# q and k of a decoder layer projected once to 128 rows, their 96-row stacks made on TensorE by selection matrices

## The chip, the cores and the metric

The kernel runs on one core of a Trainium2 chip. Five engines share the work, each with an instruction queue of its own that runs in program order: PE (TensorE, matmuls into PSUM), DVE (VectorE), ACT (ScalarE), POOL (GpSimd) and SP (SyncE, which here only issues DMAs). They wait for one another by semaphores. The metric is the device time of one execution in microseconds (us); lower is better.

## What is computed

One pre-norm decoder layer on x and ctx of shape (32, 128, 128): 32 batches of 128 tokens with 128 channels. All weights and tensors are fp32.

```
x = x + proj(causal_attention(layernorm(x)))       # 16 heads of 8 channels
x = x + Wo(cross_attention(layernorm(x), ctx))     # one head of 128
x = x + moe(layernorm(x))                          # 8 experts, top 2, one shared expert

# in the first line, with f a factor by position and channel (rotary):
q, k, v = split(x @ W_attn.T + b_attn)
q, k = q * f, k * f
att = softmax(mask(q @ k.T / sqrt(8)))
```

## The kernel before

**Stages and slots.** The 32 batches go through a software pipeline. A table, ORDER, lists the stages; each row has a name, how many batches it runs ahead of (or behind) the current slot, a part, and for some the remainder of the batch by four for which alone it runs. In slot s every engine goes through the table once and issues what it has to do for each stage. The table thus sets the order on all engines. Layernorm, the transposes of x, the projections of q and k and the routing are done for a group of four batches (512 tokens) at a time: group g's projections in slot 4g-2, its routing 11 slots behind. So the slots come in four kinds. In this text slot A is the one with the projections (s mod 4 = 2), B the next (which ends with the routing's `ranks`), then C and D (which has the layernorm of the next group on POOL). Behind the pipeline come the expert layers, from about 385 us on; the change does not touch them.

**q and k before.** A score needs products of fp32 precision from a faster format of 4 bytes with fewer bits (fp32r). Each value is therefore split into a rounded half (hi) and the rest (lo), and a head's 8 channels become 24 rows: hi, hi, lo for q against hi, lo, hi for k. Four heads make a stack of 96 rows (KR), and there are four stacks (NJ) for q and four for k. Before the change the three copies come from the weights: `wqk_hi` and `wqk_lo` hold every weight column three times.

- `project` (PE L636): eight per group, n = 0 to 7, each three matmuls (hi x hi, hi x lo, lo x hi) of 96 rows by 512 tokens into one of the four shared PSUM banks. DVE (L1090) adds the bias and multiplies by the factor into `t_qk`.
- `stacks` (ACT L884): one copy per batch, `t_qk` to `qk_stack`, which rounds.
- `stack_lo` (DVE L1101): two instructions per batch that turn the lo rows into t - hi. Then SP issues eight DMAs that spread the stacks of k and q into `k_slots` and `q_slots` (L415, L421), for which the score matmuls wait.

**Around it, per batch.** `scores` (PE L654, L655; DVE L1113 takes the row maximum), `turn_max`, `scores_t` (PE L670; ACT L896 takes the exponential; POOL L566 masks the result), `values` (PE L680, 32 small matmuls), `tall_sums` (PE L688 transposes, after ACT L902), `turn_y` (PE L694), `attn_out`, then the cross-attention (`turn_x2`, `xproject`, `xscores`, `turn_xprobs`, `xout`) and the norm for the experts (POOL L552, L554; PE L736).

**Banks.** The four shared PSUM banks are used in turn by all these stages. A stage names its bank in the table BANK; PE waits with `bank_free` until the last use of that bank has been read, and the reading engine counts it in `bank_drained`. Two stages with one bank that follow each other therefore wait for a copy.

## Time and profile before

| | |
|---|---|
| time, median of 3 runs | 591.26 us (588.47 to 596.85) |
| profiled execution, as a whole | 590.25 us |
| its span, first to last instruction | 588.3 us |
| mean granted clock of PE | 0.916 of full speed |
| start up to slot 2 | 0 to about 50 us |
| pipeline, with a period of 44.4 us per group from 123 us on | 50 to about 385 us |
| expert layers | 385 to 588 us |

The profile lists per engine the busy time, groups of instructions with their mean duration, the waits with the engine that ended them, and the chain of work that ended last. A matmul's duration has its latency in it; what one costs in a row of many is the distance from one start to the next, here called its pitch.

### The profile page before, as it was taken

What the parts mean: (1) busy time and instruction counts of PE and PEld (TensorE: products, weight loads), DVE (VectorE), ACT (ScalarE), POOL (GpSimd) and SP (SyncE); (2) the same over time, 40 slices, a digit from 0 to 9 for tenths busy, and PEclk for the clock granted to TensorE, in tenths of its full rate; (3) what the DMA queues carried; (4) which work ended last, traced back from release to release, by engine and by line L of the source; (5) the groups of instructions that cost most, each with busy time, mean ns of one, the idle gap of its engine ahead of it and who ended that gap; (6) DMA issues with size and microseconds to landing.
All of it is one profiled execution on the core that took longest, in us unless ns stands there. A gap on an engine that the chain in (4) does not pass through costs nothing.

```text
span 588.3 us, 12877 instructions
## 1 busy us (share of the span) xinstructions
PE 478.2 (81%) x3398; PEld 358.6 (61%) x3398; DVE 440.6 (75%) x1291; ACT 304.3 (52%) x927; POOL 352.0 (60%) x465
## 2 busy tenths in 40 slices
PE   4638899997887987987977987655699999999994
PEld 4415666665665655655755765434577777777783
DVE  4698989999889889889879875577446666556575
ACT  1213776856746746746746766534134444444440
POOL 7313575745767767767767786865135555555552
PEclk9959999998998998998998997956989999999997
DMA  7312121221221221221221220511112222222185
GB/s 207 96 46 54 45 60 47 59 58 33 62 60 46 60 61 48 59 62 48 57 66 46 62 75 10 172 55 58 55 47 79 79 74 74 79 70 78 55 261 174
DMA packets 66780, 43.15 MB, mean 73 GB/s; under 512 B 9020, under 2 KB 63656, under 8 KB 66712
## 3 DMA queue, kind: packets, MB, share of 16 engines
q1 hardware_dynamic: 61654, 33.01, 22.1%
q0 software_dynamic: 4320, 8.99, 4.6%
q8 instruction: 32, 0.52, 0.4%
q10 hardware_dynamic: 738, 0.33, 0.2%
q14 instruction: 36, 0.29, 0.2%
HBM read 17.36 MB, written 12.09 MB: 50 GB/s over the span
## 4 chain that ended last, share of the span: by engine, by line
PE 55%; DVE 16%; issue 12%; POOL 7%; SPq 4%; ACT 4%; DMA 2%; DVEq 0%; POOLq 0%; ACTq 0%
PE ps_scores L811 9%; PE ps_shared L636 8%; PE ps_shared L680 5%; PE ps_shared L828 4%; PE ps_scores L654 3%; PE ps_scores L655 3%; PE ps_scores_t L670 2%; PE ps_shared L819 2%; PE ps_scores_t L765 2%; POOL probs L566 2%; PE ps_scores L765 2%; PE ps_shared L779 2%; POOL xs L559 2%; SPq L415 2%; PE ps_shared L699 1%
## 5 line engine op out<-in xcount | busy, mean ns | idle before, releaser
L566 POOL TENSOR_SCALAR_AFFINE_SELECT probs<-probs 128x512 f32<-128x512 f32 x128 | 91.8, 736 | 62.1 <-ACT probs L896 60.9
L586 POOL DMA_INDIRECT ys<-ctx_t,t_qk x71 | 68.5, 965 | 75.6 <-ACT ctx_t L994 71.5
L1113 DVE TENSOR_REDUCE negmax<-ps_scores 128x4 f32<-128x512 f32 x128 | 82.6, 679 | 8.8 <-PE ps_scores L655 8.7
L559 POOL DMA_INDIRECT xs<-xrow,posu x64 | 70.6, 1104 | 19.6 <-issue 11.9
L896 ACT ACTIVATE probs<-ps_scores_t 128x512 f32<-128x512 f32 x128 | 72.8, 593 | 18.3 <-PE ps_scores_t L670 18.0
L655 PE MATMUL ps_scores<-k_slots,qk_stack 96*128 96x512 f32 x128 | 77.4, 634 | 0.0
L811 PE MATMUL ps_scores<-wide,qk_stack 128*128 x213 | 69.9, 438 | 7.0 <-DVE vst L1300 2.9
L654 PE MATMUL ps_scores<-causal,ident 128*128 128x512 bf16 x128 | 53.1, 415 | 14.0 <-DMA k_slots<-qk_stack 11.8
L1306 DVE COPY probs<-ps_shared 128x256 f32<-128x256 f32 x71 | 30.1, 424 | 45.6 <-issue 22.9
L670 PE MATMUL ps_scores_t<-wide,qk_stack 97*128 97x512 f32 x128 | 61.7, 508 | 0.3 <-ACT probs L896 0.2
L1101 DVE SCALAR_TENSOR_TENSOR qk_stack<-qk_stack,lo_rows,t_qk 96x512 fp32r<-96x512 f32 x64 | 58.6, 953 | 1.7 <-ACT qk_stack L884 1.7
L1090 DVE SCALAR_TENSOR_TENSOR t_qk<-ps_shared,bqk,ropes 96x512 f32<-96x512 f32 x64 | 45.5, 743 | 8.4 <-PE ps_shared L636 8.3
L811 PEld LDWEIGHTS ps_scores<-wide,qk_stack 128*128 128x128 f32 x213 | 36.4, 193 | 23.0 <-issue 19.0
L989 ACT ACTIVATE vst<-ps_scores 128x256 f32<-128x256 f32 x71 | 27.3, 384 | 42.5 <-PE ps_scores L811 40.1
L680 PE MATMUL ps_shared<-probs,vst 128*32 128x128 f32 x1024 | 35.8, 281 | 14.9 <-issue 13.9
L828 PE MATMUL ps_shared<-wd,probs 128*128 x284 | 43.8, 277 | 0.1
L680 PEld LDWEIGHTS ps_shared<-probs,vst 128*32 128x32 f32 x1024 | 27.5, 113 | 22.2 <-issue 22.1
L902 ACT ACTIVATE yu<-ps_shared 128x512 f32<-128x512 f32 x32 | 19.1, 598 | 37.7 <-PE ps_shared L680 37.7
L984 ACT ACTIVATE qk_stack<-ps_scores_t 128x128 fp32r<-128x128 f32 x71 | 19.7, 278 | 35.9 <-PE ps_scores_t L803 24.3
L884 ACT ACTIVATE qk_stack<-t_qk 96x1024 fp32r<-96x1024 f32 x32 | 33.3, 1044 | 9.1 <-DVE t_qk L1090 9.1
L828 PEld LDWEIGHTS ps_shared<-wd,probs 128*128 128x128 f32 x284 | 37.7, 193 | 0.3 <-issue 0.3
L1300 DVE SCALAR_TENSOR_TENSOR vst<-vst,t_qk,ps_scores 128x256 f32<-128x256 f32 x71 | 33.5, 471 | 2.2 <-ACT vst L989 2.2
(227 smaller groups left out, 1222.0 us busy)
## 6 DMA issues: line engine op xcount, KB each, us to landing
k_slots<-qk_stack SPq DMA_DIRECT2D x128, 48.0 KB
wide<-qk_stack SPq DMA_DIRECT2D x128, 48.0 KB
t_qk<-xs SPq DMA_DIRECT2D x71, 66.0 KB
wide<-ys SPq DMA_DIRECT2D x8, 512.0 KB, 7.9
ctx_t<-in_ctx SPq DMA_DIRECT2D x32, 64.0 KB, 2.1
out_x<-res SPq DMA_DIRECT2D x8, 256.0 KB, 3.1
ys<-ctx_t,t_qk POOLq DMA_INDIRECT x71
wd<-in_L_ffn_w_down SPq DMA_DIRECT2D x8, 128.0 KB, 3.3
```

What stands on the lines that cost most here:

```text
L559: pool.indirect_dma_start(out=xs, out_offset=bass.IndirectOffsetOnAxis(ap=posu[:, g % 2, k, u:u + 1], axis=0), in_=xrow[:, g % 2, k, u, :] ...
L566: pool.affine_select(out=part, in_=part, compare_op=ALU.is_ge, fill=0.0, base=0, pattern=[[0, HJ], [1, T]], channel_multiplier=-1).then_in ...
L586: pool.indirect_dma_start(out=ys, out_offset=bass.IndirectOffsetOnAxis(ap=xload_i[:, i % XL, C + 1:C + 2], axis=0), in_=ybuf[:, i % 4, :], ...
L654: pe.matmul(PS[j % 2][:], ident16[:], causal[:].rearrange("p a t -> p (a t)"), start=True, stop=False)
L655: pe.matmul(PS[j % 2][:], qk_stack[0:KR, b % 4, j, :], k_slots[:, b % 2, j].rearrange("p a t -> p (a t)"), start=False, stop=True)\
L670: pe.matmul(PT[j % 2][:], qk_stack[0:KR + 1, b % 4, NJ + j, :], q_slots[:, b % 4, j].rearrange("p a t -> p (a t)"), start=True, stop=True) ...
L680: mm = pe.matmul(bank[VW * i:VW * (i + 1), j * T:(j + 1) * T], vst[:, b % 4, h, :], probs[:, b % 2, h, :], start=True, stop=True, skip_gro ...
L811: mm = pe.matmul(PS[i % 2][:], a[:, i % 4, :], m[:, bass.ds(e, 1), :].rearrange("p a f -> p (a f)"), start=(r == 0), stop=(r == 2))
L828: mm = pe.matmul(PM[i % 2][:, 0:C], xhT[:, i % 3, f * 128:(f + 1) * 128], wd[:, bass.ds(e, 1), f, :].rearrange("p a c -> p (a c)"), start= ...
L896: act.activation(probs[:, b % 2, j * HJ:(j + 1) * HJ, :].rearrange("p a t -> p (a t)"), PT[j % 2][:], ACT.Exp)\
L1101: ins = dve.scalar_tensor_tensor(out=part, in0=part.bitcast(fp32), scalar=lo_rows[:, k:k + 1], in1=t_qk[0:KR, cs, u * T:(u + 1) * T], op0= ...
L1113: dve.reduce_max(negmax[:, b % 2, j * HJ:(j + 1) * HJ], PS[j % 2][:].rearrange("p (i t) -> p i t", i=HJ), axis=AX.X, negate=True).then_inc ...
```

## The change

q and k are projected once, to 128 rows each (16 heads by 8 channels): two projections per group instead of eight. DVE adds the bias and multiplies by the factor as before, now 128 rows at a time. The new stage `halves` splits the result for the whole group: ACT copies it rounded to `qk_hi`, DVE subtracts to `qk_lo`. The new stage `select` makes the stacks on PE: for a pair of batches (256 tokens) and each quarter j of the rows, two matmuls for q and two for k multiply 32 rows of `qk_hi` and `qk_lo` by constant matrices of zeros and ones (`picks`), which place every channel in its three rows. ACT copies the bank to `qk_stack`, which has six places now instead of four. `stacks` and DVE's part of `stack_lo` are gone; SP's part waits for the copies of `select`. Pair 0 of a group is selected in slot A, pair 1 in slot B. The weights are no longer tripled at the start; DVE makes `picks` there instead, and one more DMA is issued.

```diff
 ORDER = [
     ("turn_x", 2, None, 0),
     ("turn_ffn", -7, None, None),
-    ("stacks", 1, None, 0),
     ("rstd_x", 3, None, 0),
     ("scores_t", -2, 2, None),
     ("turn_max", -1, None, None),
+    ("project", 2, 0, 0),
     ("scores_t", -2, 3, None),
+    ("project", 2, 1, 0),
     ("xscores", -5, None, None),
     ("router", -7, None, None),
...
     ("project_v", 1, None, 2),
+    ("halves", 2, 0, 0),
     ("turn_y", -3, None, None),
-    ("project", 2, 5, 0),
+    ("halves", 2, 1, 0),
...
     ("values", -2, None, None),
-    ("project", 2, 1, 0),
-    ("project", 2, 3, 0),
     ("project_v", 2, None, 3),
-    ("project", 2, 6, 0),
+    ("select", 2, 0, 0),
+    ("select", 3, 0, 2),
+    ("select", 2, 1, 0),
+    ("select", 3, 1, 2),
...
-        "router": 1, "turn_x2": 0, "ranks": 0, "project": (0, 1, 1, 3, 3, 3, 2, 2)}
+        "router": 1, "turn_x2": 0, "ranks": 0, "project": (1, 3), "select": (1, 3, 2, 0)}
...
             def stack_lo(b):
 
-                w.ge(stacked, b + 1)
+                for j in range(NJ):
+                    w.bank_read(("select", b // 2 * 2, j))
...
             def project(g, n):
 
-                col = (n + NJ) % (2 * NJ)
+                col = 1 - n
...
-                    mm = pe.matmul(bank[0:KR, :], a[:, col, :], m[:, 0, :], start=(k == 0), stop=(k == 2))
+                    mm = pe.matmul(bank[:], a[:, col, :], m[:, 0, :], start=(k == 0), stop=(k == 2))
                 mm.then_inc(put_bank(("project", g, n)), 1)
+
+            def select(b, j):
+                bank = w.bank_free(("select", b, j))
+                w.ge(qk_split, 2 * (b // GB + 1))
...
+                r, cs = slice(32 * j, 32 * (j + 1)), slice(b % GB * T, (b % GB + 2) * T)
+                for k in range(2):
+                    part = bank[0:KR, k * 2 * T:(k + 1) * 2 * T]
+                    for n, m in enumerate((qk_hi, qk_lo)):
+                        mm = pe.matmul(part, picks[r, k, n].rearrange("p i a d -> p (i a d)"), m[r, k, cs], start=(n == 0), stop=(n == 1))
+                mm.then_inc(put_bank(("select", b, j)), 1)
...
-            def stacks(b):
-
-                u = b % GB
-                w.bank_read(("project", b // GB, 7))
-                w.ge(scored_t, NJ * (b - 3))
-                act.activation(qk_stack[0:KR, b % 4], t_qk[0:KR, :, u * T:(u + 1) * T], ACT.Copy).then_inc(rounded, 1)
+            def halves(g, n):
+                w.bank_read(("project", g, n))
+                for j in range(NJ):
+                    w.bank_read(("select", GB * g - 2, j))
+                act.activation(qk_hi[:, 1 - n, :], qk[:, 1 - n, :], ACT.Copy).then_inc(rounded[n], 1)
+
+            def select(b, j):
+
+                bank, drain = w.bank_filled(("select", b, j))
+                w.ge(scored_t, NJ * (b - RING + 2))
+                s = b % RING
+                act.activation(qk_stack[0:KR, s:s + 2, j::NJ, :].rearrange("p u k t -> p k u t"),
+                               bank[0:KR, :].rearrange("p (k u t) -> p k u t", k=2, u=2), ACT.Copy).then_inc(drain, 1)
...
+            def halves(g, n):
+                w.bank_read(("project", g, n))
+                w.ge(rounded[n], g + 1)
+                for j in range(NJ):
+                    w.bank_read(("select", GB * g - 2, j))
+                dve.tensor_tensor(qk_lo[:, 1 - n, :], qk[:, 1 - n, :], qk_hi[:, 1 - n, :].bitcast(fp32), ALU.subtract).then_inc(qk_split, 1)
+
             def stack_lo(b):
-
-                u = b % GB
-                w.ge(rounded, b + 1)
-                for k, cs in enumerate((slice(0, NJ), slice(NJ, 2 * NJ))):
-                    part = qk_stack[0:KR, b % 4, cs, :]
-                    ins = dve.scalar_tensor_tensor(out=part, in0=part.bitcast(fp32), scalar=lo_rows[:, k:k + 1],
-                                                   in1=t_qk[0:KR, cs, u * T:(u + 1) * T], op0=ALU.mult, op1=ALU.add)
-                ins.then_inc(stacked, 1)
```

Quarters 2 and 3 of `select` stand in ORDER where `project` 0 and 4 stood, around `xproject` and `scores_t`. Some tensors share memory now (`early`, `late`); no stage moves by that.

**PE, start of a slot A.** In these rows `xn1` and `early` are the normalized x, `ps_shared0` to `ps_shared3` the four banks, and the brackets name the semaphores waited for. Before:

```order
L624 MATMUL ps_shared2<-ident,xn1 128x128 x3
L736 MATMUL ps_shared1<-ident,xrow 128x128 [waits xn3_ready,bank_drained1]
L670 MATMUL ps_scores_t0<-wide,qk_stack 128x512 [waits exped]
L662 MATMUL ps_shared3<-ident,negmax 16x128 [waits maxed,bank_drained3]
L670 MATMUL ps_scores_t1<-wide,qk_stack 128x512 [waits exped]
L719 MATMUL ps_shared2<-xcT,qa 128x128 [waits bank_drained2]
L741 MATMUL ps_shared1<-wrT,x3T 128x9 [waits bank_drained1]
L654 MATMUL ps_scores0<-causal,ident16 128x512 [waits k_slotted2,maxed]
L655 MATMUL ps_scores0<-k_slots,qk_stack 128x512
L694 MATMUL ps_shared1<-ident,yn 128x128 [waits bank_drained0,bank_drained1]
L636 MATMUL ps_shared3<-xT_hi,wqk_hi 96x512 [waits xT_split,bank_drained3]
```

The same place of the change:

```order
L626 MATMUL ps_shared2<-ident,early 128x128 x3
L750 MATMUL ps_shared1<-ident,xrow 128x128 [waits xn3_ready,bank_drained1]
L684 MATMUL ps_scores_t0<-wide,qk_stack 128x512 [waits exped]
L676 MATMUL ps_shared3<-ident,negmax 16x128 [waits maxed,bank_drained3]
L638 MATMUL ps_shared1<-xT_hi,wqk_hi 128x512 [waits xT_split,bank_drained1]
L638 MATMUL ps_shared1<-xT_lo,wqk_hi 128x512
L638 MATMUL ps_shared1<-xT_hi,wqk_lo 128x512
L684 MATMUL ps_scores_t1<-wide,qk_stack 128x512 [waits exped]
L638 MATMUL ps_shared3<-xT_hi,wqk_hi 128x512 [waits xT_split,bank_drained3]
L638 MATMUL ps_shared3<-xT_lo,wqk_hi 128x512
L638 MATMUL ps_shared3<-xT_hi,wqk_lo 128x512
L733 MATMUL ps_shared2<-xcT,qa 128x128 [waits bank_drained2]
```

The first matmul that waits for the split x (`xT_split`) stood behind `turn_y` (L694) and stands now two stages behind the transposes of x, ahead of the cross-attention scores (L719, now L733).

**PE, end of a slot A.** From the score matmuls to the transposes of the sums (L688, now L702). Before, where a projection is one row of its three:

```order
L655 MATMUL ps_scores1<-k_slots,qk_stack 128x512
L636 MATMUL ps_shared0<-xT_hi,wqk_hi 96x512 [waits xT_split,bank_drained0]
...
L712 MATMUL ps_shared2<-xcT,wA 128x128 [waits bank_drained0,bank_drained2]
L713 MATMUL ps_shared2<-wM,xcT 128x128
L670 MATMUL ps_scores_t0<-wide,qk_stack 128x512 [waits q_slotted1,max_placed,exped]
L636 MATMUL ps_shared3<-xT_hi,wqk_hi 96x512 [waits xT_split,bank_drained3]
...
L730 MATMUL ps_shared3<-cm,xprobsT 128x128 [waits bank_drained1,bank_drained3]
L670 MATMUL ps_scores_t1<-wide,qk_stack 128x512 [waits exped]
L688 MATMUL ps_shared0<-ident,yu 128x128 [waits bank_drained0]
```

The same place of the change, of each quarter's four matmuls the first two:

```order
L669 MATMUL ps_scores1<-k_slots,qk_stack 128x512
L650 MATMUL ps_shared2<-qk_hi,picks 96x256 [waits qk_split,bank_drained2]
L650 MATMUL ps_shared2<-qk_lo,picks 96x256
...
L726 MATMUL ps_shared2<-xcT,wA 128x128 [waits bank_drained0,bank_drained2]
L727 MATMUL ps_shared2<-wM,xcT 128x128
L684 MATMUL ps_scores_t0<-wide,qk_stack 128x512 [waits q_slotted1,max_placed,exped]
L650 MATMUL ps_shared0<-qk_hi,picks 96x256 [waits qk_split,bank_drained0]
L650 MATMUL ps_shared0<-qk_lo,picks 96x256
...
L744 MATMUL ps_shared3<-cm,xprobsT 128x128 [waits bank_drained1,bank_drained3]
L684 MATMUL ps_scores_t1<-wide,qk_stack 128x512 [waits exped]
L702 MATMUL ps_shared0<-ident,late 128x128 [waits bank_drained0]
```

The third quarter fills bank 2, and the next stage, `xproject` (L726), waits for bank 2; the fourth fills bank 0, for which the transposes (L702) wait two stages later. A slot B has the same rows now.

**DVE, start of a slot A.** Before:

```order
L1083 TENSOR_TENSOR xT_lo<-xT,xT_hi 128x512 [waits xhi_done,bank_drained2]
L1144 TENSOR_REDUCE xneg<-ps_shared2 128x1 [waits bank_drained2,bank_filled2]
L1165 MAX mx8<-ps_shared1 128x8 [waits bank_filled1]
L1168 MAX_INDEX ix8<-mx8,ps_shared1 128x8 [waits topped]
L1101 SCALAR_TENSOR_TENSOR qk_stack<-qk_stack,lo_rows,t_qk 96x512 [waits rounded]
L1113 TENSOR_REDUCE negmax<-ps_scores0 128x4 [waits bank_drained3,scored]
L1090 SCALAR_TENSOR_TENSOR t_qk<-ps_shared3,bqk,ropes 96x512 [waits stacked,bank_filled3]
```

The same place of the change:

```order
L1106 TENSOR_TENSOR xT_lo<-early,xT_hi 128x512 [waits xhi_done,bank_drained2]
L1112 SCALAR_TENSOR_TENSOR early<-ps_shared1,bqk,ropes 128x512 [waits bank_filled1]
L1112 SCALAR_TENSOR_TENSOR early<-ps_shared3,bqk,ropes 128x512 [waits bank_filled3]
L1165 TENSOR_REDUCE xneg<-ps_shared2 128x1 [waits bank_drained2,bank_filled2]
L1186 MAX mx8<-ps_shared1 128x8 [waits bank_filled1]
L1189 MAX_INDEX ix8<-mx8,ps_shared1 128x8 [waits topped]
L1134 TENSOR_REDUCE negmax<-ps_scores0 128x4 [waits bank_drained3,scored]
L1122 TENSOR_TENSOR qk_lo<-early,qk_hi 128x512 [waits bank_drained3,bank_drained2,bank_drained1,bank_drained0,rounded0]
```

Both bias adds of the group (L1112) stand now between the split of x and the row maximum of the cross-attention (L1144, now L1165) and the router's index (L1168, now L1189), which PE's `turn_y` waits for through its bank; the stack adds (L1101) are gone.

## Rows read from the trace of the kernel before

**Rows 1.** The page, busy us, share of the span and instructions by engine

```profile
PE 478.2 (81%) x3398; PEld 358.6 (61%) x3398; DVE 440.6 (75%) x1291; ACT 304.3 (52%) x927; POOL 352.0 (60%) x465
```

**Rows 2.** Slots A to D of one group, all engines; columns below

```profile
204.80:220.70 15.90, 12.87 (x97) 9.29 (x96) 12.44 (x29) 7.11 (x22) 10.71 (x16) 1.00 0.24 60
220.70:231.20 10.50, 7.22 (x70) 5.10 (x68) 9.67 (x36) 7.75 (x23) 8.78 (x12) 0.97 0.19 48
231.20:240.70 9.50, 9.40 (x71) 7.13 (x72) 8.86 (x39) 6.27 (x19) 4.78 (x7) 0.68 0.21 53
240.70:249.20 8.50, 7.45 (x72) 5.46 (x71) 7.16 (x20) 6.71 (x24) 7.78 (x9) 1.00 0.24 60
```

The columns are from:to, length, busy us (instructions) of PE, PEld, DVE, ACT and POOL, PE's granted clock, the DMA share and GB/s.

**Rows 3.** The chain that ended last: start, us, engine, output, line, count

```profile
217.89 2.11 PE ps_shared L636 x9
```

**Rows 4.** PE in order of time: start, us, operation, [idle before, its end]

```profile
222.65 0.33 PE L694 MATMUL ps_shared<-ident,yn 128*128 128x128 f32 x1 [0.21 <-DVE ix L1168]
...
224.88 1.08 PE L680 MATMUL ps_shared<-probs,vst 128*32 128x128 f32 x32 [0.31 <-issue]
...
231.26 0.18 PE L747 MATMUL ps_shared<-selb,tri 128*128 128x32 bf16 x1 [2.70 <-DVE cum L1191]
...
251.48 0.30 PE L736 MATMUL ps_shared<-ident,xrow 128*128 128x128 f32 x1 [1.58 <-POOL xrow L554]
251.88 0.48 PE L670 MATMUL ps_scores_t<-wide,qk_stack 97*128 97x512 f32 x1
...
256.63 1.08 PE L680 MATMUL ps_shared<-probs,vst 128*32 128x128 f32 x32 [1.28 <-issue]
```

**Rows 5.** The same chain further on, in another group

```profile
329.19 0.44 PE ps_shared L688 x4
```

**Rows 6.** Groups by line and shape, whole span: busy us, mean ns, idle before

```profile
L614 PE MATMUL ps_shared<-woT,probs 128*128 128x128 f32 x2 | 0.8, 501 | 0.3 <-DVE wpT L1051 0.3
L616 PE MATMUL ps_shared<-rows,one_row 1*128 1x128 f32 x2 | 0.8, 497 | 0.0
L636 PEld LDWEIGHTS ps_shared<-xT_lo,wqk_hi 128*96 128x96 f32 x64 | 10.7, 168 | 3.5
L1101 DVE SCALAR_TENSOR_TENSOR qk_stack<-qk_stack,lo_rows,t_qk 96x512 fp32r<-96x512 f32 x64 | 58.6, 953 | 1.7 <-ACT qk_stack L884 1.7
L1090 DVE SCALAR_TENSOR_TENSOR t_qk<-ps_shared,bqk,ropes 96x512 f32<-96x512 f32 x64 | 45.5, 743 | 8.4 <-PE ps_shared L636 8.3
L884 ACT ACTIVATE qk_stack<-t_qk 96x1024 fp32r<-96x1024 f32 x32 | 33.3, 1044 | 9.1 <-DVE t_qk L1090 9.1
L902 ACT ACTIVATE yu<-ps_shared 128x512 f32<-128x512 f32 x32 | 19.1, 598 | 37.7 <-PE ps_shared L680 37.7
```

**Rows 7.** DVE in order of time, start of the next slot A

```profile
252.00 0.68 DVE L1083 TENSOR_TENSOR xT_lo<-xT,xT_hi 128x512 fp32r<-128x512 f32 x1
```

**Rows 8.** All engines in order of time, 339 to 351 us

```profile
339.95 2.15 DVE L1101 SCALAR_TENSOR_TENSOR qk_stack<-qk_stack,lo_rows,t_qk 96x512 fp32r<-96x512 f32 x2
...
340.66 1.94 POOL L566 TENSOR_SCALAR_AFFINE_SELECT probs<-probs 128x512 f32<-128x512 f32 x2
...
348.87 1.22 POOL L566 TENSOR_SCALAR_AFFINE_SELECT probs<-probs 128x512 f32<-128x512 f32 x2
```

**Rows 9.** SP's DMA issues in order of time, 28 to 70 us

```profile
29.53 3.47 SPq L415 DMA_DIRECT2D k_slots<-qk_stack  x4
...
35.51 0.78 SPq L421 DMA_DIRECT2D wide<-qk_stack  x1
38.43 3.25 SPq L415 DMA_DIRECT2D k_slots<-qk_stack  x4
...
56.76 3.25 SPq L421 DMA_DIRECT2D wide<-qk_stack  x4
...
62.12 0.57 SPq L429 DMA_DIRECT2D wide<-max_rows  x1
63.30 3.71 SPq L415 DMA_DIRECT2D k_slots<-qk_stack  x4
```

More of the change, by code:

```diff
@@ L603, in _ @@
             pe.transpose(PM[1][:, 0:C], wsq[:, 4, :], ident[:])
-            pe.wait_ge(dve_step, 1)
-            for k in range(2 * NJ):
-                pe.matmul(PM[1][0:KR, 2 * C + k:2 * C + k + 1], brow[:, k, :], one_row[:, 0:1], start=True, stop=True)
             pe.transpose(PM[1][:, C:C + NE], wr[:], ident[0:NE, 0:NE]).then_inc(filled[1], 1)
@@ L901, in values @@
                 w.bank_read(("tall_sums", b - 1))
[L902 removed]
+                act.activation(yu, bank[:], ACT.Copy).then_inc(drain, 1)
             def turn_y(b):
```

132 lines of the change are left out of this document (68 added, 64 removed).

## The prediction, made before the change had run

> **What bounds it now.** I read the page's busy line first [rows 1]: PE is busy for 81% of the span and DVE for 75%, so neither is full, and the share alone tells nothing. Then the span by stretches. From 123 to 301 us the same pattern returns every 44.4 us, once per group of four batches, so I cut one group into its four slots [rows 2]: A (15.9 us, which holds all eight projections), B (10.5, which holds the routing), C (9.5) and D (8.5). DVE is the engine with the most work in the group (12.44 + 9.67 + 8.86 + 7.16 = 38.1 of 44.4 us). The change takes about 10 us of that away, and the question is what those 10 us now hold up.
>
> The chain that ended last and the waits of PE give the answer, slot by slot. In A, PE runs its projections back to back [rows 3], and its two long waits are 1.58 us at the start, for POOL's normalized rows, and 1.28 us before the values matmuls [rows 4]; there POOL's mask of the probabilities is the late one. In B it waits 0.21 us for DVE and 0.31 us before the values, and then 2.70 us for the running counts of the routing, a chain of small DVE instructions [rows 4]. C has no wait of note: PE is busy for 9.40 of 9.5 us, at a mean granted clock of 0.68, that is, partly at the lower level of 1.2 GHz after the 2.70 us of idleness [rows 2]. In D POOL is busy for 7.78 of 8.5 us [rows 2]. So DVE lies on the chain with short latencies and not with its total, and the two stages that the change takes from it, the add of the bias and the second half of the stacks, are hardly on it.
>
> **PE's work.** A projection costs 2.11 / 9 = 0.234 us per matmul of 512 columns [rows 3]. A group loses 18 of its 24, 4.2 us, all in slot A. It gains 32 matmuls of 256 columns (two pairs of batches, four quarters, four matmuls each), 16 in A and 16 in B. No row has 256 columns. From below: 128 columns take 0.44 / 4 = 0.11 us [rows 5]. From above: on the straight line between 0.11 and 0.234 they take 0.15. Half of the 512-column price is 0.117, so I take 0.13: 2.1 us in A, 2.1 us in B, 4.2 per group, between 3.5 and 4.8. That they multiply only 32 rows should make no difference: a matmul over one row (L616) took 497 ns where one over 128 rows (L614) took 501 [rows 6]. So PE's total stays as it is, but 2.1 us move from A to B.
>
> One price could be much worse, that of the weight loads, since each of the 32 matmuls has a matrix of its own. The projections show loads of 96 columns of 168 ns each [rows 6], and yet a pitch of 0.234, which leaves no room for them: they ran under the matmul ahead. The Trainium skill, "TensorE: Matmul & The Clock Gate", Part 3, The mechanism, says that a weight load overlaps a running matmul only where the two use different row groups. By that rule all four matmuls of a quarter, which share one row group, would pay their loads openly. The trace does not agree for the projections, which fill all rows and still hide theirs.
>
> **New waits in A and B.** (i) The projections now stand near the start of A. Their input, the low half of x, is ready at 252.00 + 0.68 = 252.68 [rows 7], while PE would reach the first at 251.88 [rows 4]: 0.8 us of wait, and queued behind it are score matmuls and the cross-attention scores. (ii) DVE's two bias adds (743 ns each [rows 6]) now stand ahead of the row maximum and the router's index, for which the next transpose on PE waits. I put this wait at 0.8 instead of 0.2, so +0.6; nothing if PE is late itself, 1.5 if both adds are waited for in full. (iii) The third quarter and the next stage, xproject, use the same PSUM bank, with nothing between them. PE must wait until the matmul has drained (about 0.25, since a matmul of 512 columns is 0.48 us long [rows 4] at a pitch of 0.234) and ACT has copied the bank, 598 ns for 128x512 [rows 6]: 0.85 us. (iv) The fourth quarter and the transposes of the sums share a bank too; between them PE has 0.45 us of work, but ACT has an exponential ahead of the copy, so 0.65 us. (v) The 1.28 us that A waits for POOL goes: PE now comes later than POOL.
>
> Slot A: -4.2 + 2.1 + 0.8 + 0.6 + 0.85 + 0.65 - 1.3 = -0.5 us. Slot B: + 2.1 + 0.85 + 0.65, less the 0.5 of its two short waits (0.21 and 0.31), which are gone when DVE and POOL have less to do there: +3.1 us. The 2.70 of the routing stay, since that chain begins behind the transposes and is not touched. C stays: nobody is waited for.
>
> **What DVE's relief gives.** It shows in one place. With the stack add beside it (339.95 to 342.10 us) a pair of POOL's masks takes 1.94 us; in the next slot, where there is none, 1.22 [rows 8]. In D POOL is the bound, and one such pair lies on the chain: -0.7 us. The remaining 8 adds of 953 ns and 6 of 743 per group were covered by PE. What replaces them on DVE (two adds, two subtractions of about 0.7) lies in A.
>
> ACT trades four copies of 1.04 us for two of 0.6 and eight of 0.6 [rows 6], +1.8 us per group. It is busy for 7.11 of 15.9 us in A and 7.75 of 10.5 in B [rows 2], so this is hidden but for (iii) and (iv); without the cover it would cost 11 us over six groups.
>
> **The first slots.** Up to 80 us the issues of SP bound the kernel, 8 copies per batch of 0.8 us each. SP lies idle from 36.29 (35.51 + 0.78) to 38.43, until DVE has added batch 1's stack, and from 60.01 to 62.12 and 62.69 to 63.30 [rows 9]. The stacks of two batches now come together and early, without DVE: 2.1 + 2.7 = about -5 us. The first issue at 29.53 moves little (a shorter weight split, but four drained banks to wait for). Behind the last group, slot 30 gains the 0.7 us of POOL.
>
> **Sum.** Seven groups have an A and a B with this work; the first lies in the stretch that SP bounds. Six groups from slot 6 on: 6 x (-0.5 + 3.1 - 0.7) = +11.4; start -5; end -0.7; together +5.7. The profiled execution took 590.25 us as a whole (span 588.3), 1.0 under the median of 591.26; 590.25 + 5.7 gives 596.
>
> **Rivals.**
> *Faster: DVE was the bound after all.* The relief would then show in every slot and not in D alone, and the waits (i) and (ii) would be absorbed. Price: 0.7 more in A, B and C each, and 0.8 + 0.6 in A; 3.5 per group, 21 in all less what B counts already (0.5 x 6): 18, so 578. For it: DVE has the most work of all in the group, and POOL's pair shows that it disturbs others. Against: only short DVE pieces lie on the chain. It decides from two further slots on that shorten by 0.7.
> *Slower: the drains are longer.* If ACT has one earlier copy in hand when the third or fourth quarter is full, each of the four waits per group grows by 0.6: 2.4 x 6 = 14 more, 610. For it: copies of two quarters and the values stand right ahead. Against: by my count ACT is free some 0.3 us before. It decides once these waits pass 1.2 us.
> *Slower: the loads are in the open.* 32 x 0.168 = 5.4 us per group, over all seven groups 38 more: 634. For it speaks that 256 columns (0.12 us) are shorter than a load of 168 ns; against it, that transposes of 128 columns, with loads of 128 columns, keep a pitch of 0.11 [rows 5]. The rule of the Trainium skill named above would lead here.
>
> **Chances.** The forecast has 0.56, with a range of its own from 588 to 604. The faster rival has 0.2, the longer drains 0.16, the open loads 0.08. Two per cent, which is about what a measurement of this kernel can tell from no change, is 579.4 to 603.1. Most of the faster rival lies under it (0.17); both slower ones lie above, with a little of the forecast's tail (0.25); 0.58 remains. The range from 579 to 613 takes in the bounds of the 256-column price (0.7 x 6 = 4 us either way) and of (ii), and leaves out the open loads and half of the faster rival.
>
> **What would show it.** In the profile after: slot B of a group grows from 10.5 to some 13.6 us, A and C keep their lengths, D loses 0.7. PE's idle time ahead of xproject and of the transposes of the sums ends with ACT's copies of the stacks, at about 0.85 and 0.65 us. The matmuls with the selection matrices start 0.13 us apart. SP has no gap of 2 us at 36. DVE's load per group falls to about 28 us. The prediction is wrong if B keeps its length (the drains are hidden), if C falls below 9 us, or if the granted clock drops in A or B ahead of the routing, for which no row here gives a price.

## The result, and the profile after

| | before | the change |
|---|---|---|
| median, side by side on one chip | 591.73 us (4 runs) | 606.69 us (603.88 to 610.03, 4 runs) |
| profiled execution, as a whole | 590.25 us | 603.88 us |
| its span | 588.3 us | 602.1 us |

The ratio is 1.025, with an interval from 1.015 to 1.034: slower, by 15 us, though the first comparison alone does not tell whether by more than 2 per cent. A second one, on another chip, gave 609.43 against 593.08, 1.033 (1.025 to 1.040). Medians are those of all executions, while ratios leave out the ones that lie in a slower state. The forecast was 596 with a range of its own from 588 to 604, and 579 to 613 over all cases. The time lies in the wide range and outside the narrow one.

The line of the profile that answers to [rows 1], busy us, share of the span and instructions by engine, of the change:

```profile
PE 492.3 (82%) x3494; PEld 365.1 (61%) x3494; DVE 368.7 (61%) x1198; ACT 321.4 (53%) x975; POOL 335.4 (56%) x465
```

DVE is busy for 72 us less and PE for 14 us more, although PE's work was to stay as it is (at the lower clock a matmul of 512 columns is 0.63 us long and not 0.40, and the change has more of that, see below).

For the comparison by slots I cut at the transposes of the expert norm (L736 before, L750 after), which are easy to find in both traces. First a group of before on this cut, slots A, B, C, D; the columns are those of [rows 2]; the clock is the third number from the end.

```profile
251.48:265.08 13.60, 12.17 (x90) 8.79 (x91) 12.12 (x28) 5.35 (x18) 8.51 (x12) 1.00 0.22 56
265.08:275.73 10.65, 7.31 (x73) 5.24 (x72) 9.83 (x36) 7.70 (x23) 8.78 (x12) 0.96 0.18 47
275.73:285.11 9.38, 9.35 (x71) 7.04 (x70) 8.74 (x39) 6.33 (x20) 4.77 (x7) 0.68 0.22 55
285.11:295.82 10.71, 8.09 (x76) 5.90 (x75) 7.43 (x22) 8.42 (x27) 9.94 (x13) 1.00 0.25 64
```

The same view of the change, two of its groups:

```profile
168.12:182.43 14.31, 12.82 (x89) 9.28 (x90) 8.62 (x24) 8.81 (x24) 8.21 (x12) 0.82 0.21 55
182.43:197.40 14.97, 11.97 (x89) 8.48 (x89) 7.48 (x32) 8.51 (x24) 8.29 (x12) 0.73 0.16 44
197.40:205.79 8.39, 8.36 (x69) 6.33 (x69) 7.22 (x35) 5.38 (x19) 4.24 (x7) 0.77 0.18 49
...
262.57:275.75 13.18, 10.96 (x88) 7.37 (x89) 8.52 (x24) 8.74 (x24) 8.25 (x12) 1.00 0.21 57
275.75:288.42 12.67, 9.61 (x90) 6.62 (x88) 7.54 (x31) 8.29 (x25) 8.29 (x12) 1.00 0.18 48
288.42:299.05 10.63, 9.00 (x71) 6.84 (x69) 7.93 (x37) 5.36 (x19) 4.24 (x7) 0.68 0.21 57
299.05:309.04 9.99, 8.10 (x77) 5.91 (x76) 5.50 (x20) 7.59 (x26) 9.21 (x13) 1.00 0.20 54
```

and slot A of its other groups from 120 us on:

```profile
120.01:135.61 15.60, 12.52 (x90) 8.61 (x89) 8.92 (x24) 9.75 (x27) 5.93 (x10) 0.89 0.18 48
215.77:229.83 14.06, 12.67 (x89) 8.91 (x90) 8.62 (x24) 8.81 (x24) 8.29 (x13) 0.83 0.19 51
309.04:323.62 14.58, 12.51 (x89) 8.64 (x89) 8.48 (x24) 8.73 (x24) 8.20 (x12) 0.88 0.18 49
```

Before, all groups are alike. After, they differ, and the granted clock tells which is which. In the second group A and B run at the full 2.4 GHz: A is 0.42 us shorter than before, B 2.02 longer. In the first one the clock is 0.82 in A and 0.73 in B, and they are 0.7 and 4.3 longer, but C is 1.0 shorter there and 1.2 longer in the second: B and C together are 23.36 and 23.30. D is 0.7 shorter.

The waits of PE over three groups of the change (168 to 307 us): us in total, times, longest.

```profile
PE ps_shared L761 <- DVE cum L1212: 6.5, 3, 2.2
PE ps_shared L750 <- POOL xrow L555: 4.7, 3, 1.6
PE ps_shared L726 <- ACT qk_stack L904: 4.1, 6, 0.7
PE ps_shared L708 <- DVE ix L1189: 2.5, 4, 1.6
PE ps_shared L638 <- DVE xT_lo L1106: 2.2, 3, 0.7
PE ps_shared L694 <- issue: 1.0, 3, 0.3
```

Lines three and five are new: `xproject` waits for the copy of the third quarter, 0.68 us in every slot A and B; the first projection for the split of x, 0.7 us once per group. `turn_y` waited for the router's index before, too, for 1.5 us over three groups, now for 2.5. The wait ahead of the values (L694, before L680), 7.5 us over three groups before, is 1.0.

Where the clock falls is seen in stretches of 1 us, at the start of the slot A from 215.77 us (first two) and at its end (last two):

```profile
217.77:218.77 1.00, 1.00 (x5) 0.82 (x4) 0.68 (x1) 0.45 (x1) 0.83 (x2) 0.74 0.04 8
218.77:219.77 1.00, 1.00 (x5) 0.81 (x5) 0.31 (x2) 0.15 (x1) 0.97 (x2) 0.50 0.19 49
...
227.77:228.77 1.00, 1.00 (x7) 0.60 (x5) 0.12 (x1) 1.00 (x3) 0.31 (x1) 0.86 0.00 0
228.77:229.77 1.00, 1.00 (x5) 0.85 (x5) 0.71 (x3) 0.69 (x2) 0.36 (x2) 0.50 0.00 0
```

Ahead of the first fall PE had waited 1.56 us for POOL and 0.71 for the split of x; ahead of the second, 0.68 for the third quarter's copy. Then it works at 1.2 GHz (0.50) though it has no idle time. Added up over 100 to 350 us, the granted clock was at the lower level for 34 us before (one stretch per group, behind the routing) and for 61 us after (up to three per group); in the profile of the second comparison it was 48. That the waits bring the fall about is a guess at this point.

### The profile page after: what moved, and what is told of

It is laid out like the page before. It is cut to its first block, busy times and chain, and to the rows that moved or that the text cites. A ratio compares the mean times of both kernels' runs of the same rounds, so it can differ in the third digit from the quotient of the medians.

```text
span 602.1 us, 13119 instructions
## 1 busy us (share of the span) xinstructions
PE 492.3 (82%) x3494; PEld 365.1 (61%) x3494; DVE 368.7 (61%) x1198; ACT 321.4 (53%) x975; POOL 335.4 (56%) x465
## 4 chain that ended last, share of the span: by engine, by line
PE 62%; DVE 12%; ACT 7%; issue 7%; POOL 5%; DMA 3%; SPq 3%; DVEq 0%; ACTq 0%; POOLq 0%
PE ps_scores L825 10%; PE ps_shared L694 5%; PE ps_scores_t L684 4%; PE ps_shared L842 4%; PE ps_scores L668 4%; PE ps_shared L650 4%; PE ps_scores L669 4%; PE ps_shared L638 3%; ACT qk_stack L904 3%; PE ps_shared L702 2%; PE ps_scores L779 2%; PE ps_shared L833 2%; PE ps_scores_t L779 2%; PE ps_shared L726 2%; PE ps_shared L793 1%
## 5 line engine op out<-in xcount | busy, mean ns | idle before, releaser
L567 POOL TENSOR_SCALAR_AFFINE_SELECT probs<-probs 128x512 f32<-128x512 f32 x128 | 81.8, 653 | 72.4 <-ACT probs L917 71.9
L1134 DVE TENSOR_REDUCE negmax<-ps_scores 128x4 f32<-128x512 f32 x128 | 85.2, 686 | 46.6 <-PE ps_scores L669 46.2
L590 POOL DMA_INDIRECT ys<-ctx_t,late x71 | 68.4, 964 | 72.5 <-ACT ctx_t L1015 69.8
L560 POOL DMA_INDIRECT xs<-xrow,posu x64 | 66.8, 1044 | 19.7 <-issue 11.8
L684 PE MATMUL ps_scores_t<-wide,qk_stack 97*128 97x512 f32 x128 | 64.8, 529 | 0.5 <-issue 0.3
L694 PE MATMUL ps_shared<-probs,vst 128*32 128x128 f32 x1024 | 37.2, 289 | 4.0 <-issue 3.3
L904 ACT ACTIVATE qk_stack<-ps_shared 96x512 fp32r<-96x512 f32 x64 | 35.8, 592 | 7.8 <-PE ps_shared L650 7.6
L1175 DVE SCALAR_TENSOR_TENSOR res<-ps_shared,xinv,late 128x128 f32<-128x128 f32 x32 | 11.2, 350 | 43.5 <-PE ps_shared L744 42.7
L545 POOL TENSOR_SCALAR xn<-late,mv,rs 128x128 f32<-128x128 f32 x32 | 25.4, 793 | 21.7 <-ACT rs L934 21.6
L923 ACT ACTIVATE late<-ps_shared 128x512 f32<-128x512 f32 x32 | 19.1, 597 | 30.3 <-PE ps_shared L694 30.3
L694 PEld LDWEIGHTS ps_shared<-probs,vst 128*32 128x32 f32 x1024 | 28.1, 115 | 11.3 <-issue 8.9
L573 POOL TENSOR_TENSOR late<-late,bias 128x128 f32<-128x128 f32 x32 | 14.6, 456 | 35.9 <-DVE late L1155 35.6
```

Of the source, the lines that this page charges most:

```text
L560: pool.indirect_dma_start(out=xs, out_offset=bass.IndirectOffsetOnAxis(ap=posu[:, g % 2, k, u:u + 1], axis=0), in_=xrow[:, g % 2, k, u, :] ...
L567: pool.affine_select(out=part, in_=part, compare_op=ALU.is_ge, fill=0.0, base=0, pattern=[[0, HJ], [1, T]], channel_multiplier=-1).then_in ...
L590: pool.indirect_dma_start(out=ys, out_offset=bass.IndirectOffsetOnAxis(ap=xload_i[:, i % XL, C + 1:C + 2], axis=0), in_=ybuf[:, i % 4, :], ...
L684: pe.matmul(PT[j % 2][:], qk_stack[0:KR + 1, b % RING, NJ + j, :], q_slots[:, b % 4, j].rearrange("p a t -> p (a t)"), start=True, stop=Tr ...
L694: mm = pe.matmul(bank[VW * i:VW * (i + 1), j * T:(j + 1) * T], vst[:, b % 4, h, :], probs[:, b % 2, h, :], start=True, stop=True, skip_gro ...
L904: act.activation(qk_stack[0:KR, s:s + 2, j::NJ, :].rearrange("p u k t -> p k u t"), bank[0:KR, :].rearrange("p (k u t) -> p k u t", k=2, u ...
```

## The experiments

All comparisons are with the kernel before on the same chip; "the change" stands at 606.7 in the expectations.

**Banks of the third and fourth quarter.** Nothing then fills these banks before ACT has copied them.

```diff
-        "router": 1, "turn_x2": 0, "ranks": 0, "project": (1, 3), "select": (1, 3, 2, 0)}
+        "router": 1, "turn_x2": 0, "ranks": 0, "project": (1, 3), "select": (1, 3, 1, 1)}
```

> The third and fourth quarter of select fill bank 1 (free since the first quarter was copied) in place of banks 2 and 0, so that neither xproject nor the transposes of the sums wait for a copy of a quarter; all else as in the change. Theory A, the drains: of the 606.7 us, each pair of quarters costs 0.68 us ahead of xproject and 0.31 ahead of the transposes of the sums, 2.0 us per group, and these go: 7 x 2.0 = 14 less, 593. Theory B, the clock: the short waits also bring TensorE's granted clock down in slots A and B; then the low stretches that begin behind xproject's wait (about 180 and 228 us in the profile of the change) go as well and the time falls below 590. Theory C, ACT is the limit of this section (its copies, the exponential and the two copies of xproject follow each other without a gap from 273.7 to 275.2 us): the wait only moves, to the exponential or to the next use of bank 1, and less than 5 us are gained, 602 or more.

Measured: 594.67 us, ratio 0.998 (0.993 to 1.002). So two numbers brought back 12 us by the medians and some 16 by the ratios; single executions run from 586.3 to 599.9, and the profiled one is the slowest. Slots A, B, C of one group:

```profile
258.65:271.46 12.81, 11.94 (x87) 8.44 (x89) 8.27 (x23) 8.46 (x24) 8.25 (x12) 0.87 0.21 59
271.46:283.59 12.13, 9.39 (x88) 6.64 (x88) 7.64 (x32) 8.52 (x25) 8.32 (x12) 1.00 0.18 50
283.59:294.14 10.55, 9.13 (x71) 6.80 (x70) 7.95 (x37) 5.39 (x19) 4.24 (x7) 0.68 0.22 59
```

Slot B is 11.8 to 12.1 us in the five groups from 120 us on, at a clock of 0.98 or more. Against the 12.67 of the change at full clock that is 0.5 less: the 0.68 ahead of `xproject` are gone, and the wait for the routing is 0.2 longer (2.4 us against 2.2). Against the change's other groups (13.5 to 15.0) it is 1.3 to 2.8 less, and these falls of the clock in B are gone, as theory B has it. But they had cost little: B and C together are 22.5 to 23.4 us in all five groups of the change, whether the clock fell in B or not, since C is the shorter behind a fall. Here they are 20.4 to 22.7. In the mean over these groups B and C give 1.4 us and A 1.3 (14.3 to 13.1), 2.7 per group, against the 2.0 of theory A. The time does not decide between theory A (593) and theory B (below 590): 12 us back make 594.7 and 16 make 590.7. The slots show the direct waits as the larger part. Theory C, ACT as the limit, falls. The low stretch in slot A stays (0.87 here, in three of five groups), so the drains are not its cause.

**The projections behind the router.**

```diff
-    ("project", 2, 0, 0),
     ("scores_t", -2, 3, None),
-    ("project", 2, 1, 0),
     ("xscores", -5, None, None),
     ("router", -7, None, None),
+    ("project", 2, 0, 0),
+    ("project", 2, 1, 0),
...
-        "router": 1, "turn_x2": 0, "ranks": 0, "project": (1, 3), "select": (1, 3, 2, 0)}
+        "router": 1, "turn_x2": 0, "ranks": 0, "project": (0, 3), "select": (1, 3, 2, 0)}
```

> The two projections stand behind the router and use banks 0 and 3 in place of 1 and 3, so that PE reaches them after the cross-attention scores, when the split of x is done; all else as in the change. Theory A, direct waits alone: the 0.74 us for the split of x go, and of the 0.60 for the router's index 0.4: 1.1 per group, 7 groups: 8 less, 599. Theory B, the clock: in the change the first low stretch of slot A begins right behind these waits (218 us); without them the granted clock of slot A is 1.00 in all groups, which gives up to 1 us more per group: 592. Against both: the halves come later, and the first quarter waits for DVE's qk_lo by up to 1 us; then nothing is gained, 605 to 608.

Measured: 597.07 us, ratio 1.008 (1.004 to 1.011), 9.6 us less than the change. Slots A and B of two groups:

```profile
261.16:273.21 12.05, 10.76 (x88) 7.58 (x90) 8.67 (x24) 8.62 (x24) 8.49 (x12) 1.00 0.22 61
273.21:285.87 12.66, 9.61 (x88) 6.62 (x88) 7.52 (x31) 8.26 (x25) 8.28 (x12) 0.97 0.18 50
305.29:318.00 12.71, 11.51 (x88) 8.41 (x89) 8.80 (x24) 8.76 (x24) 8.45 (x12) 0.91 0.21 56
318.00:332.88 14.88, 11.88 (x87) 8.46 (x88) 7.37 (x30) 8.45 (x24) 8.29 (x12) 0.73 0.16 42
```

At full clock A is 12.05 us, against 13.18: the 1.1 of theory A, to the tenth. Theory B was too bold: A has 1.00 in two of five groups, 0.91 in the other shown and 0.83 in another, and where the clock holds out in A it can still fall in B, where the drains are untouched (14.88 at 0.73).

**Both edits.** No new lines.

> The edits of the banks (bank 1 for the third and fourth quarter) and of the projections (behind the router, banks 0 and 3) together. Apart they gave 12.0 and 9.6 us of 606.7. If each takes away a wait of its own and the low stretch of the clock behind it, they add up: 585, and slots A and B show a granted clock of 0.95 or more. If the low stretch is brought about by what is left (the wait for POOL's row at the start of a slot A, that of the routing), it stays, and the two together give 590 to 593.

Measured: 588.32 us, ratio 0.997 (0.993 to 1.001): 18 of the 22 us that they gave apart. B is 11.8 to 12.1 at 1.00 throughout, but A still has a low stretch in three of five groups, here in that from 209.66 us:

```profile
209.66:221.74 12.08, 11.82 (x88) 8.47 (x90) 8.20 (x23) 8.43 (x24) 8.21 (x12) 0.86 0.22 59
```

The only wait that the trace shows in that slot is the 1.56 us for POOL's row. Before the change the same wait stood at the same place [rows 4], and the clock of A stayed at 1.00. Why it falls now is not settled: in these rows the slot differs in more than one thing. What the two edits gained lies nearly all in A (11.8 us in the mean over five groups, 14.3 in the change); B and C together are 22.2 to 22.9.

**All quarters on the same rows.** Quarters two to four repeat the first here, so this kernel computes something else.

```diff
-                r, cs = slice(32 * j, 32 * (j + 1)), slice(b % GB * T, (b % GB + 2) * T)
+                r, cs = slice(0, 32), slice(b % GB * T, (b % GB + 2) * T)
```

> All four quarters of select read rows 0 to 31, so that the other three stacks repeat the first (the scores of twelve heads are then those of other heads); shapes, banks and order are those of the change. In the change the eight matmuls of the first two quarters took 0.65 us, hardly longer than four of one quarter. If that is because matmuls over different 32 rows run at once, the eight now take as long as two quarters one behind the other, 0.9 us or more, and the starts of the two quarters no longer coincide. If it is the ordinary pitch of 256 columns, the eight still take 0.65 us.

One execution: 622.08 us, of which about 6 come from a later start (its third group begins at 86.8 and not 80.8 us; the start is treated below). The select matmuls of the first two quarters, first in the change, PE in order of time:

```profile
269.90 0.37 PE L650 MATMUL ps_shared<-qk_hi,picks 32*96 32x256 f32 x2
...
270.33 0.29 PE L650 MATMUL ps_shared<-qk_lo,picks 32*96 32x256 f32 x2
270.56 0.39 PE L668 MATMUL ps_scores<-causal,ident 128*128 128x512 bf16 x1
```

and the same place with all quarters on rows 0 to 31:

```profile
285.46 0.35 PE L650 MATMUL ps_shared<-qk_hi,picks 32*96 32x256 f32 x1
285.65 0.28 PE L650 MATMUL ps_shared<-qk_lo,picks 32*96 32x256 f32 x1
...
286.36 0.28 PE L650 MATMUL ps_shared<-qk_lo,picks 32*96 32x256 f32 x1
```

In the change the matmuls of both quarters start in pairs (x2: one of each, less than 0.02 us apart), the last pair 0.43 us after the first, and eight take 0.66 us up to the next matmul (269.90 to 270.56). On the same rows they start one by one, 0.12 apart behind the first two, and the eighth starts 0.90 after the first. So matmuls over different 32 rows run side by side. The Trainium skill states this ("TensorE: Matmul & The Clock Gate", Why this matters for your kernels: small-K matmuls in distinct row groups run concurrently); the trace agrees, for two of four groups. The rule on loads that I had weighed instead does not show even on the same rows, where each matmul has a load of its own and the pitch stays 0.12. The groups of this kernel are 2.5 us longer than those of the change; two such places per group, 0.47 us each, account for 0.9. For the rest no wait was singled out; in the four groups from 128 us on the clock is at the lower level for 75 us, against 51 in four groups of the change.

**The selection matrices later.** The lines that make `picks` move unchanged.

```diff
-            dve.memset(picks[:].bitcast(fp32), 0.0)
-            step(dve.reduce_sum(quarter[:], ident[:].rearrange("p (j r) -> p r j", j=NJ), axis=AX.X))
...
             dve.memset(rsum[:], 0.0).then_inc(setup_done, 1)
+            dve.memset(picks[:].bitcast(fp32), 0.0)
+            step(dve.reduce_sum(quarter[:], ident[:].rearrange("p (j r) -> p r j", j=NJ), axis=AX.X))
```

> DVE makes the selection matrices behind the preparation of the weights, not ahead of it; all else as in the change. If the 3.95 us that these five instructions take ahead of the weights hold up the start (the first projection began at 21.06 us, before the change at 18.80, although it has fewer projections to wait for), the first projection starts at about 18 us, SP's first copy at about 27 and not at 29.75, and the time falls by 2.5 to 4 us, to 603. If the start is bound by something else (loads of x, the constants), SP's first copy stays within 0.5 us and the time stays at 606 to 607.

Measured: 609.29 us, ratio 1.029 (1.023 to 1.034): nothing gained, and the first projection is at 23.0 us, not at 18. The profile shows why the case is not that simple. DVE at the start, in order of time, first in the change and then with the banks edited, where the start is the same program:

```profile
7.16 0.29 DVE L1061 COPY probs<-cols 128x256 f32<-128x256 f32 x1 [1.68 <-DMA ropes<-in_rotary]
...
10.31 3.40 DVE L1069 CAST picks<-quarter 128x64 fp32r<-128x64 f32 x4
```

```profile
7.64 4.34 DVE L1061 COPY probs<-cols 128x256 f32<-128x256 f32 x1 [2.13 <-DMA ropes<-in_rotary]
...
14.84 2.16 DVE L1069 CAST picks<-quarter 128x64 fp32r<-128x64 f32 x4
```

and POOL in the profile with the banks edited:

```profile
7.34 1.04 POOL L486 TENSOR_TENSOR early<-early,rs 128x512 f32<-128x512 f32 x1
8.32 3.51 POOL L512 MEMSET k_slots<- 96x4096 f32 x1
```

The same copy of DVE from SBUF to SBUF takes 0.29 us in the one and 4.34 in the other, where it ends (11.98) when POOL's memset does (11.83). It is held by POOL unless it comes first: of the thirteen profiles of the change and its variants, five have it ahead of that TENSOR_TENSOR of POOL, and it takes 0.29 or 0.30 us; in seven it starts behind, and takes 4.3 to 4.6; in the fast version below, where the memsets come later, it starts behind as well and takes 0.95. The copies of `picks` meet the same memsets. The Trainium skill describes it ("SBUF — State Buffer", Who interferes with whom: a copy of DVE in a two-port mode and GpSimd lock each other out for whole instructions); the trace agrees, and adds that the loser can wait through two of POOL's instructions in a row. So the start of the change depends on which engine comes first: the first projection is at 21.1 us in its own two profiles, at 24.8 with the banks or the projections edited, where SP's first copy is 4 to 6 us later too (33.6 and 35.7 against 29.75). Before the change, DVE's only such copies ahead of the weights lay in front of POOL's memsets in the trace. Moving the matrices alone does not remove this: with them moved, the copy L1061 took 4.33 us.

**POOL's memsets behind the matrices**, twice, and the change once more beside the second:

```diff
             norm_x_rows(0)
+            pool.wait_ge(picked, 1)
             const(pool.memset(k_slots[:].bitcast(fp32), 0.0))
```

> POOL waits at the start until DVE has made the selection matrices, ahead of its three long memsets; all else as in the change. In the change DVE's copies into them (L1069) took 3.40 us, from 10.31 to 13.71, beside POOL's memsets (8.30 to 13.7); in the profiles of the moved matrices, the banks and the projections the copy L1061 took 4.3 to 4.5 us beside the same memsets and the first projection came 2 to 3 us later still. Theory A, POOL's memsets hold DVE's copies up and these the weights: the copies take 0.3 us each or less, the first projection starts at 18 us or before, SP's first copy comes at 27 us, and the time falls by 3 to 6 us, to 601 to 604. Rival: POOL's memsets of k_slots, now later, bind SP's first copy, or the gain is lost in the slots up to 80 us: less than 1.5 us.

> POOL's memsets behind DVE's matrices once more, since the first time left it open: its profile had the first projection at 18.73 us and SP's first copy at 27.42, 2.3 us before those of the change, and the median was 606.05 against 606.69. If the start is worth what its profile shows, the median lies 2 to 4 us under that of the change on the same chip. If the slots up to 80 us or the clock's low stretches take it back, the two differ by less than 1.5 us.

> The change once more, beside the next run on the same chip. If the start is fixed from run to run, its first projection begins at 21 us as in the first profile; if it depends on whether DVE's copy L1061 slips in ahead of POOL's memsets (7.16 us in the first profile, 7.6 in those of the banks and the projections, where it then took 4.3 us), the first projection is seen at about 24 us in some profiles, and single times differ by some 5 us. Median 604 to 609.

Measured: 606.05 and 606.28 us. The change beside the second of them: 609.43. The mechanism is plain in the profile of the first; DVE again:

```profile
7.21 0.30 DVE L1062 COPY probs<-cols 128x256 f32<-128x256 f32 x1 [1.60 <-DMA ropes<-in_rotary]
...
10.37 0.47 DVE L1070 CAST picks<-quarter 128x64 fp32r<-128x64 f32 x4
```

The four copies take 0.47 us in place of 3.40, the first projection starts at 18.7 and 18.9 us, SP's first copy at 27.4 and 27.6 in place of 29.8. What it is worth in time stays open: 0.6 us by the medians, as the rival had it, and 3.2, as theory A had it, with intervals that overlap those of the change. By the profiles the third group of batches, whose transposes of x stand at 80.82 and 81.85 us in the change, begins at 79.31 and 80.82: of the 2.3 us 1.0 to 1.5 are left there. The change's two profiles, both with the better start, were the fastest of their executions (603.88, 602.09), which fits a start that is worse in the others, but the others have no trace.

**DVE's load put back.**

```diff
             def stack_lo(b):
...
+                for k in range(2):
+                    ins = dve.scalar_tensor_tensor(out=spare[0:KR, k], in0=ropes[0:KR, k:k + 1, 0:112].broadcast_to([KR, 4, 112]), scalar=bqk[0:KR, k:k + 1],
+                                                   in1=bias1[0:KR, 0:112].rearrange("p (a t) -> p a t", a=1).broadcast_to([KR, 4, 112]), op0=ALU.mult, op1=ALU.add)
```

> The change with DVE's old load put back: at the place of stack_lo two instructions per batch of the old kind (multiply and add of 96 rows by 448 columns, in a spare place, from constants), for which nothing waits; the output does not use them. Some 0.85 us each, 54 us in all. If the relief of DVE gave 0.7 us per group (POOL's pair of masks in slot D) and nothing else, the time grows by 5 us, to 611. If DVE's total was a bound of its own, it grows by 15 or more. If the relief is worth nothing, 606 to 608.

Measured: 615.91 us, ratio 1.042 (1.036 to 1.049), 9.2 more than the change. In slot D, POOL in the change and then here:

```profile
301.72 1.22 POOL L567 TENSOR_SCALAR_AFFINE_SELECT probs<-probs 128x512 f32<-128x512 f32 x2
```

```profile
313.51 1.80 POOL L568 TENSOR_SCALAR_AFFINE_SELECT probs<-probs 128x512 f32<-128x512 f32 x2
```

The masks take 1.80 us beside the load and 1.22 without, and slot D is 10.56 us and not 9.99; so are the slots behind the last group (8.4 and 8.1 against 7.8 and 7.5). Six slots D from 112 us on and the one behind them come to 4.2 us. Slots A to C show no price: in the mean over five groups they are 37.3 us together, in the change 37.4. Of the 14.1 us by which this profile is longer, 7.4 lie ahead of the third group (88.21 us, in the change 80.82); the start was the worse one here (first projection at 24.85 us), so what the load costs there is not told apart. In the groups DVE's relief is thus worth what it frees on POOL and no more.

**A faster version.** Both edits, the fourth quarter directly behind the third (banks 1 and 0), DVE copying the second and the fourth quarter, POOL's memsets behind the matrices; then without the edit of the start, and with all copies on ACT.

```diff
     ("select", 3, 2, 2),
+    ("select", 2, 3, 0),
+    ("select", 3, 3, 2),
     ("xproject", -4, None, None),
     ("scores_t", -1, 0, None),
-    ("select", 2, 3, 0),
-    ("select", 3, 3, 2),
...
-        "router": 1, "turn_x2": 0, "ranks": 0, "project": (1, 3), "select": (1, 3, 2, 0)}
+        "router": 1, "turn_x2": 0, "ranks": 0, "project": (0, 3), "select": (1, 3, 1, 0)}
...
+            def select(b, j):
+                if j not in (1, 3):
+                    return
...
+                dve.tensor_copy(qk_stack[0:KR, s:s + 2, j::NJ, :].rearrange("p u k t -> p k u t"),
+                                bank[0:KR, :].rearrange("p (k u t) -> p k u t", k=2, u=2)).then_inc(drain, 1)
```

> A version meant to be faster than both kernels: the edits of banks and projections, the fourth quarter directly behind the third (banks 1 and 0) so that its matmuls run beside them over other rows, DVE instead of ACT copying the second and the fourth quarter, and POOL's memsets of the start behind DVE's matrices. By the sum: 606.7 - 12.0 - 9.6 (banks and projections), - 0.45 us for each of 14 pairs that run side by side, some 6 (one pair saved 0.45 us against the run in which all quarters read the same rows), - 3 at the start: 576. If ACT or the clock is what is left over, 583 to 588. If DVE's copies delay the row maxima, 590 or more.

> The fast version without its edit of the start. If the start is worth 2 to 6 us on a kernel whose groups do not wait for the quarters, 579 to 583; if it is worth nothing there either, 576 to 578.

> The fast version with all four copies of the quarters on ACT as in the change. If the side by side quarters and the free banks are what makes it fast, 576 to 579. If ACT's queue would be the next limit (it has yu, three copies and the two of xproject in a row), xproject's and the exponential's results come 0.6 to 1.2 us later in slots A and B: 583 to 590.

Measured: 576.73 us, ratio 0.978 (0.973 to 0.984), faster than both kernels, by about 2 per cent than the one before. Without the edit of the start 579.93, 0.981 (0.974 to 0.988); with ACT's copies 578.98, 0.978 (0.971 to 0.985). The three do not differ beyond their intervals: DVE's copies gain nothing that shows, and the start at most a few us. Slots A to D of the fast version:

```profile
239.97:251.19 11.22, 11.02 (x87) 8.08 (x89) 9.28 (x25) 7.14 (x22) 7.57 (x11) 0.85 0.24 65
251.19:263.15 11.96, 8.77 (x88) 6.21 (x88) 9.16 (x34) 7.58 (x24) 8.86 (x13) 1.00 0.19 52
263.15:274.20 11.05, 9.38 (x70) 6.98 (x70) 7.95 (x37) 5.37 (x19) 4.23 (x7) 0.69 0.22 58
274.20:284.19 9.99, 8.08 (x76) 5.91 (x75) 5.49 (x20) 7.57 (x26) 9.21 (x13) 1.00 0.19 52
```

Slot A is 2.4 us shorter than before, D 0.7; B and C together are still 3.0 longer.

## Why the prediction was right and wrong

**Right, and by its mechanism: the waits.** PE in the second group shown:

```profile
267.24 0.33 PE L708 MATMUL ps_shared<-ident,yn 128*128 128x128 f32 x1 [0.60 <-DVE ix L1189]
...
272.00 0.27 PE L650 MATMUL ps_shared<-qk_lo,picks 32*96 32x256 f32 x1
272.96 0.49 PE L726 MATMUL ps_shared<-xcT,wA 128*128 128x128 f32 x2 [0.68 <-ACT qk_stack L904]
...
274.72 0.47 PE L684 MATMUL ps_scores_t<-wide,qk_stack 97*128 97x512 f32 x1
275.26 0.66 PE L702 MATMUL ps_shared<-ident,late 128*128 128x128 f32 x4
...
291.79 0.47 PE L708 MATMUL ps_shared<-ident,yn 128*128 128x128 f32 x1 [1.63 <-DVE ix L1189]
```

(i) The wait for the split of x is 0.74 us there, forecast 0.8. (ii) `turn_y` waits 0.60 in A, forecast 0.8. (iii) The third quarter's last matmul starts at 272.00 and `xproject` at 272.96; less the pitch of 0.12 that is a hole of 0.84 us (0.68 of it behind the matmul's end), forecast 0.85. (v) POOL's 1.28 us are gone. **D** was forecast at -0.7 and is 10.71 against 9.99; the experiment with the load confirms why. B and C together were forecast at +3.1 and are +3.3 in this group (23.30 against 20.03) and +3.0 in the mean over the five groups from 120 us on.

**Right in sum, not in place: C.** "C stays" failed, though C's mean over five groups is that of before. In the second group shown, `turn_y` waits 1.63 us in C for the router's index, which stands on DVE behind the routing. Before, PE ran the start of C at 1.2 GHz and came no earlier than the index. B took 1.1 us less than forecast in that group, and C 1.2 more. In two groups the clock had fallen in B, and C is 8.25 and 8.39 us, below the 9 that the text had named as a sign that it is wrong.

**Mis-sized: the fourth quarter and the select matmuls.** (iv) The transposes of the sums wait 0.3, not 0.65 (274.72 to 275.26, less the pitch of 0.234). The wait for the routing, which was to stay at 2.70, is 2.2. Single select matmuls are 0.12 apart (0.13 was taken), but two quarters side by side take 0.66 and not 1.04: all a little in favour of the change.

**Wrong: slot A, where the clock was given no price.** At full clock A is -0.42, where -0.5 stood in the sum. But in the other four of the five groups it is 14.06 to 15.60 us, and the mean is +0.8 (14.3 against 13.6). A fall in A goes with 0.9 to 1.4 us more; in the first of the five groups the wait for the split of x is also 1.86 us and not 0.7. The profile of the second comparison shows the same: 13.13 and 13.16 us in the two groups at full clock, 14.30, 14.57 and 15.24 in the others, mean +0.5. The text had named a falling clock in A or B as what would make it wrong, and had no row for a price. In B the fall has no price of its own, as said of the banks: C gives it back. What brings the clock down in A is open. It still falls there in three of five groups with the banks edited, with the projections edited and with both.

**Wrong: the start at -5.** SP's copies of batch 6 begin 2.0 us earlier (79.02 before, 77.00 after), and the third group 0.9 us earlier (81.70, 80.82). The gap at 36 us closed as forecast, but the one from 60 to 63 shrank only from 2.7 us to 0.9, a new one of 0.8 stands at 67.5, and the first issue did not come earlier: the matrices, of which "a shorter weight split" took no account, stand in front of the weights on DVE, and POOL holds them up. In the profile of the second comparison nothing is gained up to the third group (81.85).

**The sum.** From the third group's start to the last one's the change takes 226.0 us (80.82 to 306.87) against 211.9 (81.70 to 293.65): five groups of +2.8 in place of +1.9, 4.6 over the forecast. The start is 4.1 over. From the last group to the end of the pipeline it is +2.5 (104.8 against 102.3 between the same transposes, 309.04 to 413.81 and 295.82 to 398.07) in place of 1.9 - 0.7, 1.3 over; and the expert layers come 1.9 the other way, which no term had. 596 + 4.6 + 4.1 + 1.3 - 1.9 = 604; the profiled execution took 603.9. It is the fastest of the four, and the 2.8 us up to the median of 606.7 are not accounted for.

So the step that failed is twofold: the start, put at -5 and found at -0.9, and slot A, put at -0.5 and found at +0.8, with a clock that the sum took to be full. The likeliest case, "within 2 per cent" with 0.58, failed with them, clearly in the second comparison (from 1.025 up) and not beyond doubt in the first (from 1.015 up); slower had 0.25. That the time lies nearer to the 610 of the second rival than to 596 is chance: its place is right, since the banks of the quarters are what 12 us could be won back from, but these waits had no more than the length that the forecast gave them, and not 1.2 us. The faster rival is refuted for the groups by the load put back, the open loads by the quarters on the same rows.

## What to carry to other kernels

A forecast for TensorE has to be priced with and without a fall of the granted clock: here the same slot took 13.2 us without and 14.1 to 14.6 with one. Add up over the next slot too, since what one loses by the clock another can give back. When work moves to another engine, the order of stages and the use of the banks have to move with it: the same change with three stages moved, two bank numbers changed and POOL's memsets later is 2 per cent faster than the kernel before, where it was 2.5 per cent slower. Relief of an engine that is not late is worth what it stops disturbing, here on POOL's masks in one slot of four, and can be tested by putting the load back with nothing waiting for it.

## What the runs showed of the hardware

Matmuls over rows 0 to 31 and 32 to 63 ran side by side although they were issued as four of the one and then four of the other: eight in 0.66 us. A 0.29 us copy of DVE took 4.34 us where POOL's instructions came first. A pair of POOL's masks took 1.80 us beside DVE's load and 1.22 without. And TensorE's granted clock fell to 1.2 GHz behind waits of 0.7 us in some groups and not in others of the same kernel; what brings it about was not settled.
